# Masked keys' weight subtracted from P, and one product per head with v's totals, in a fused attention and FFN kernel

## The reference

```
x = x + LN(attn(LN(x)))          # x: (8, 512, 1024) float32
x = x + LN(ffn(LN(x)))

attn: qkv = x @ w_qkv.T + b_qkv  # 8 heads of 64, part = 512
      scores[f, t] = k[f] . q[t]             # no scaling
      scores = where(f <= t, scores, -10000)
      attn = softmax(scores, over f)
      vals[t] = sum_f attn[f, t] * v[f]
      out = vals @ w_o.T + b_o
ffn:  x @ W.T + b, plus the low-rank product B[:, :r] A[:r] x whose rank r (8, 16, 32, 64) the gate picks
```

## Time and profile before

| | |
|---|---|
| median of 3 runs | 1454.88 us (1454.22 to 1455.05) |
| span of the profiled execution | 1453.0 us |
| TensorE busy | 1436.8 us (99%) |
| VectorE, ScalarE, GpSimd busy | 920.2, 692.4, 623.7 us |
| HBM traffic | 59 GB/s over the span |

### The profile page before, as it was taken

The page is one execution under the profiler, slowest core; times in us unless marked ns, Lnnn a source line. Parts: engine busy times, 40 slices in busy tenths (PEclk is TensorE's granted clock), DMA queues, the critical chain, the costliest instruction groups (busy, mean ns, idle before and its releaser), DMA issues.

```text
span 1453.0 us, 24689 instructions
## 1 busy us (share of the span) xinstructions
PE 1436.8 (99%) x7852; PEld 1280.6 (88%) x7852; DVE 920.2 (63%) x2118; ACT 692.4 (48%) x1497; POOL 623.7 (43%) x1154
## 2 busy tenths in 40 slices
PE   7999999999999999999999999999999999999998
PEld 6888888888888888888888889999999999999998
DVE  7576575675675775765855887655555555555554
ACT  6365465564574673654654763333333323333332
POOL 3353451461553452533622584444443344444442
PEclk9999999999999999999999999999999999999999
DMA  7212113113122122121122722322222222222211
GB/s 251 83 41 70 58 35 101 32 26 101 36 54 69 40 54 79 40 58 65 40 58 91 207 88 102 102 102 102 100 82 85 101 101 87 101 101 101 94 69 62
DMA packets 51540, 118.72 MB, mean 82 GB/s; under 512 B 5552, under 2 KB 22192, under 8 KB 51504
## 3 DMA queue, kind: packets, MB, share of 16 engines
q1 hardware_dynamic: 51504, 118.27, 25.7%
HBM read 60.06 MB, written 25.69 MB: 59 GB/s over the span
## 4 chain that ended last, share of the span: by engine, by line
PE 95%; DMA 1%; POOL 1%; DVE 1%; ACT 1%; issue 0%; POOLq 0%; DVEq 0%
PE ps_f L2036 26%; PE ps_o L1391 20%; PE ps_o L1422 12%; PE ps_o L1987 11%; PE ps_s L1443 5%; PE ps_t L1301 4%; PE ps_v L1275 4%; PE ps_o L1385 3%; PE ps_v L1276 2%; PE ps_f L2017 2%; PE ps_o L1345 1%; PE ps_x L2006 1%; PE ps_t L1391 1%; PE ps_t L1284 1%; DMA valsT<-vt 1%; POOL wagl L616 1%
## 5 line engine op out<-in xcount | busy, mean ns | idle before, releaser
L2036 PE MATMUL ps_f<-wagh,x2Th 128*128 128x364 f32 x768 | 255.1, 332 | 0.4 <-POOL wagl L616 0.4
L2036 PE MATMUL ps_f<-wagh,x2Tl 128*128 128x364 f32 x768 | 252.6, 329 | 0.0
L2036 PE MATMUL ps_f<-wagl,x2Th 128*128 128x364 f32 x768 | 252.5, 329 | 0.0
L1391 PE MATMUL ps_o<-xTh,wh 128*128 128x512 f32 x424 | 174.1, 411 | 0.0
L1391 PE MATMUL ps_o<-xTh,wl 128*128 128x512 f32 x424 | 166.8, 393 | 0.0
L1391 PE MATMUL ps_o<-xTl,wh 128*128 128x512 f32 x424 | 165.9, 391 | 0.0
L2036 PEld LDWEIGHTS ps_f<-wagh,x2Th 128*128 128x128 f32 x768 | 144.3, 188 | 2.0 <-POOL wagl L616 0.7
L2036 PEld LDWEIGHTS ps_f<-wagl,x2Th 128*128 128x128 f32 x768 | 144.7, 188 | 1.1
L2036 PEld LDWEIGHTS ps_f<-wagh,x2Tl 128*128 128x128 f32 x768 | 144.5, 188 | 0.0
L558 POOL TENSOR_TENSOR cw<-wm,cnt 128x4 f32<-128x4 f32 x64 | 12.9, 202 | 299.8 <-ACT pr L1061 299.8
L731 DVE TENSOR_TENSOR PT<-ps_t,PT 128x512 fp32r<-128x512 f32 (+1 forms) x192 | 109.6, 599 | 41.2 <-ACT PT L1026 39.2
(11 more groups left out here) (222 smaller groups left out, 3494.6 us busy)
## 6 DMA issues: line engine op xcount, KB each, us to landing
kst<-kst SPq DMA_DIRECT2D x64, 256.0 KB, 3.7
xt<-in_x SPq DMA_DIRECT2D x32, 512.0 KB, 4.0
x2r<-x2n SPq DMA_DIRECT2D x30, 512.0 KB, 2.9
xs<-in_x SPq DMA_DIRECT2D x24, 512.0 KB, 4.4
out<-x SPq DMA_DIRECT2D x23, 512.0 KB, 3.0
valsT<-vt SPq DMA_DIRECT2D x64, 128.0 KB, 2.3
vraw<-valsT SPq DMA_DIRECT2D x32, 256.0 KB, 3.4
raw<-in_wqkvT SPq DMA_DIRECT2D x12, 512.0 KB, 5.9
```

The lines of the kernel that those rows point to most:

```text
L1391: done = pe.matmul(ps[:, :], w[:, k, c:c + P], xT[:, k, :], start=(k == 0 and w is wh and xT is xTh), stop=(k == KD - 1 and w is wl), skip ...
L2036: last = pe.matmul(ps_f[:, g, 0:GW], a[:, k, :], w[:, k, cols], start=(k == 0 and a is xh and w is wagh), stop=False, skip_group_check=True)
```

## The change

The masked keys' weight is no longer laid out as blocks of P. For query t the sum over all keys of wn[t] * v[f] is wn[t] times v's total. So the visible P becomes P - wn[t], and wn[t] * total is added for all keys:

vals[t] = sum over the visible key tiles of (P[f, t] - wn[t]) * v[f] + wn[t] * sum over all f of v[f]

- `normalise` subtracts wn in its second operation (an operand from SBUF in place of the constant 1.0), and a drain stands ahead of it, since wn is made just before.
- `values` reads high rows at their visible columns only, as the low rows (512, 384, 256, 128), and ends with one product: `totals[:, h, :]` by the head's diagonal (384 columns). pv_done follows that product.
- `masked_weights`, `masked_spread`, wt_ready and wn_done go; `transpose_p`'s group 1 waits for nothing of its own.
- `diagonal` has two buffers, and waits for pv_done of the head two back.
- New, once a row: ScalarE copies v tile 0 to vsum, VectorE adds tiles 1 to 3 (ahead of each tile's low part in `v_lo`), `vsum_hi` (ACT) and `vsum_lo` (DVE) split vsum, `value_totals` (PE) multiplies ones by both parts into ps_t[1] in the middle of slot 2's first projection, `totals_hi` (ACT) and `totals_lo` (DVE) split the result.
- PT's layout becomes plain, the loop's code loses the split of projections in slots other than 2, and the kernel is built with dynamic_dma_scratch_size=1024.

```diff
             def weights(h, b):
                 pool.wait_ge(rden_ready, H + 1)
-                pool.tensor_tensor(wn[:, q, :], wm[:, q, :], rden[:, q, :], ALU.mult).then_inc(wn_done, 1)
+                pool.tensor_tensor(wn[:, q, :], wm[:, q, :], rden[:, q, :], ALU.mult)
             def diagonal(h, b):
-                pool.wait_ge(wn_done, H + 1)
-                pool.wait_ge(wt_ready, 1 + H)
-                pool.tensor_tensor(W_DIAGONAL.rearrange("p (i t) -> p i t", i=3),
+                pool.wait_ge(pv_done, H + 1)
+                pool.tensor_tensor(DIAGONALS[q].rearrange("p (i t) -> p i t", i=3),
...
             def normalise(h, b):
+                pool.drain()
                 for i in range(NT):
                     at = pr[:, q, S_OFF[i]:S_OFF[i] + (i + 1) * P]
-                    last = pool.tensor_scalar(at, at, rden[:, q, i:i + 1], 1.0, ALU.mult, ALU.mult)
+                    last = pool.tensor_scalar(at, at, rden[:, q, i:i + 1], wn[:, q, i:i + 1].bitcast(F32),
+                                              ALU.mult, ALU.subtract)
                 last.then_inc(p_ready, 1)
...
             def v_lo(t, b):
                 dve.wait_ge(v_high, 4 * b + t + 1)
+                if t > 0:
+                    dve.wait_ge(v_low, 4 * b + t)
+                    done = dve.tensor_tensor(vsum[:, :], ps_j[t % 2][:, :], vsum[:, :], ALU.add)
+                    if t == NT - 1:
+                        done.then_inc(vsum_ready, 1)
...
+            def vsum_lo(b):
+                dve.wait_ge(vsum_high, b + 1)
+                dve.tensor_tensor(vsum_l[:, :], vsum[:, :], vsum_h[:, :].bitcast(F32), ALU.subtract).then_inc(vsum_low, 1)
+
+            def totals_lo(b):
+                dve.wait_ge(totals_high, b + 1)
+                dve.tensor_tensor(totals[:, :, HD:2 * HD], ps_t[1][:, :].rearrange("p (h c) -> p h c", h=NH),
+                                  totals[:, :, 0:HD].bitcast(F32), ALU.subtract).then_inc(totals_low, 1)
...
                     if h < NH and h != BARE + 1:
                         scores_max(h, b)
+                    if h == 2:
+                        totals_lo(b)
...
-            def masked_spread(h, b):
-                act.wait_ge(t_full[1], 2 * (8 * b + h) + 2)
-                act.activation(W_SPREAD, ps_t[1][:, 0:3 * P].rearrange("p (n c) -> p n c", n=3), ACT.Copy)\
-                    .then_inc(wt_ready, 1)
+            def vsum_hi(b):
+                act.wait_ge(vsum_ready, b + 1)
+                act.activation(vsum_h[:, :], vsum[:, :], ACT.Copy).then_inc(vsum_high, 1)
+
+            def totals_hi(b):
+                act.wait_ge(totals_full, b + 1)
+                act.activation(totals[:, :, 0:HD], ps_t[1][:, :].rearrange("p (h c) -> p h c", h=NH), ACT.Copy)\
+                    .then_inc(totals_high, 1)
...
         def values(pe, h, b):
             H = 8 * b + h
             pe.wait_ge(t_lo, 3 * H + 3)
-            pe.wait_ge(wt_ready, 1 + H + 1)
             if h == 0:
                 pe.wait_ge(v_low, 4 * b + 4)
             pe.wait_ge(vals_ready, 1 + H)
             for j in range(NT):
-                pe.matmul(ps_v[:, :], v[:, j, h, :], HIGH_ROWS[j], start=(j == 0), stop=False, skip_group_check=True)
-                last = pe.matmul(ps_v[:, j * P:], v[:, j, h, :], LOW_ROWS[j], start=False, stop=(j == NT - 1),
-                                 skip_group_check=True)
-            last.then_inc(pv_done, 1)
-
-        def masked_weights(pe, h, b):
-            H = 8 * b + h
+                for rows in (HIGH_ROWS[j], LOW_ROWS[j]):
+                    pe.matmul(ps_v[:, j * P:], v[:, j, h, :], rows, start=(j == 0 and rows is HIGH_ROWS[0]), stop=False,
+                              skip_group_check=True)
             pe.wait_ge(d_ready, H + 1)
-            pe.wait_ge(t_lo, 3 * H + 2)
-            pe.matmul(ps_t[1][:, 0:3 * P], ones[:, 0:1].to_broadcast([P, P]), W_DIAGONAL,
-                      start=True, stop=True).then_inc(t_full[1], 1)
+            if h == 0:
+                pe.wait_ge(totals_low, b + 1)
+            pe.matmul(ps_v[:, 0:3 * P], totals[:, h, :], DIAGONALS[h % 2], start=False, stop=True,
+                      skip_group_check=True).then_inc(pv_done, 1)
+
+        def value_totals(pe, b):
+
+            pe.wait_ge(vsum_low, b + 1)
+            pe.wait_ge(t_lo, 3 * 8 * b + 2)
+            for part in (vsum_h, vsum_l):
+                last = pe.matmul(ps_t[1][:, :], ones[:, 0:1].to_broadcast([P, P]), part[:, :],
+                                 start=(part is vsum_h), stop=(part is vsum_l))
+            last.then_inc(totals_full, 1)
```

More of the change, by code:

```diff
@@ L235, in attention_phase @@
         PT = sb("PT", [P, ROOM * P], F32R)
+        totals = sb("totals", [P, NH, 2 * HD], F32R)
+        vsum = sb("vsum", [P, PART], F32)
+        vsum_h = sb("vsum_h", [P, PART], F32R)
+        vsum_l = sb("vsum_l", [P, PART], F32R)
         ones = sb("ones", [P, 2], F32R)
@@ L676, in gpsimd @@
             pool.memset(hold[:, 1:2], 0.0).then_inc(vals_ready, 1)
-            pool.memset(hold[:, 14:15], 0.0).then_inc(wt_ready, 1)
+            pool.memset(hold[:, 14:15], 0.0).then_inc(pv_done, 2)
             pool.memset(hold[:, 2:3], 0.0).then_inc(vals_stored, 16)
@@ L879, in body @@
                         lows(h, 1, b)
+                    if h == 1:
+                        vsum_lo(b)
                     if 1 <= h <= NH and h not in (BARE, BARE + 1):
@@ L1066, in vals_lo_part @@
                 H = 8 * b + h
-                act.wait_ge(pv_done, H + 1)
+                act.wait_ge(pv_done, H + 3)
                 act.wait_ge(vals_ready, 1 + H)
@@ L1109, in body @@
                 for h in range(SLOTS):
-                    if h >= 2:
-                        masked_spread(h - 2, b)
+                    if h == 2:
+                        totals_hi(b)
                     if h == BARE + 2:
@@ L1157, in last_body @@
                 v_hi(3, b)
+                vsum_hi(b)
                 p_hi(0, 2, b)
-                masked_spread(0, b)
+                totals_hi(b)
                 exps(2, b)
@@ L1169, in last_body @@
                 p_hi(1, 2, b)
-                masked_spread(1, b)
                 q_hi(2, b)
@@ L1181, in last_body @@
                 tile_vals_high(1)
-                masked_spread(2, b)
                 q_hi(3, b)
@@ L1190, in last_body @@
                 next_high(W.wag[0])
-                masked_spread(3, b)
                 next_high(W.wag[1])
@@ L1201, in last_body @@
                     next_high(W.wag[k])
-                masked_spread(4, b)
                 exps(6, b)
@@ L1211, in last_body @@
                 next_high(W.wag[4])
-                masked_spread(5, b)
                 for k in (5, 6):
@@ L1484, in steps @@
                 items = between(BETWEEN_LAST if last else BETWEEN, h, part, b)
-                if part == 0 and h >= 2 and len(items) == 1:
+                if part == 0 and h == 2:
                     kind, p, row, ks = items[0]
@@ L1489, in steps @@
                     step(kind, p, row, ks, last)
-                    if n == 0 and part == 0 and h >= 2:
-                        masked_weights(pe, h - 2, b)
+                    if n == 0 and part == 0 and h == 2:
+                        value_totals(pe, b)
             def turns(h, place, b):
@@ L1519, in last_body @@
             def last_body(b):
-                whole, first, second = range(W.KV), range(W.KV // 2), range(W.KV // 2, W.KV)
+                whole = range(W.KV)
                 scores(0, b)
@@ L1525, in last_body @@
                     else:
-                        tile_product(h - 5, 1, first)
-                        masked_weights(pe, h - 2, b)
-                        tile_product(h - 5, 1, second)
+                        tile_product(h - 5, 1, whole)
                     if h >= 2:
@@ L1541, in last_body @@
                         transpose_p(pe, h - 1, 2, b)
-                tile_product(3, 1, whole[:1])
-                masked_weights(pe, NH - 2, b)
-                tile_product(3, 1, whole[1:2])
+                tile_product(3, 1, whole[:2])
                 values(pe, NH - 2, b)
@@ L2040, in ffn @@
                             last_transposes(pe)
-                        if first and g == 2 and k == 2:
-                            last_weights(pe)
                         if first and g == 2 and k == KD // 2:
@@ L2118, in _ @@
             attention.tensor(pe)
-            output.tensor(pe, attention.last_transposes, attention.last_weights, attention.last_values)
+            output.tensor(pe, attention.last_transposes, attention.last_values)
 def kernel(L0_attn_x, L0_attn_w_qkv, L0_attn_b_qkv, L0_attn_w_o, L0_attn_b_o, L0_ffn_W, L0_ffn_b, L0_ffn_A,
```

51 lines of the change are left out of this document (23 added, 28 removed).

## The result

| | time, us (median) | against the kernel before, 95% interval |
|---|---|---|
| before | 1454.55 (1453.91 to 1455.05) | |
| changed | 1587.47 (1584.39 to 1589.6) | 1.0913 (1.09 to 1.0926) |

A forecast was written before the change was run, and what follows sets the result against it. TensorE's own stream bounds the kernel: 11.0 us won without waits, but waits lose 0.22 us a row, 1.5 in seven rows, plus 1.2 in the last: 2.7 slower, 1457.6 us, range 1449 to 1462.

The forecast's parts named there:

- stage 2: GpSimd's normalise(): drain and second SBUF operand make P 0.47 us later; heads 5 and 7 wait, 0.95 us a row.
- 0.08 for each operand, and 4 x 0.07 to 0.08 = 0.28 for a head: Price of normalise()'s second SBUF operand on GpSimd, from 693 ns with one such operand against 611 with none.
- Most heads have several times that in slack: Claim that P being ready 0.47 us later delays TensorE's first transposes only in heads 5 and 7.
- The stream: TensorE's values and product of a head cost 1.43 us instead of 1.67, winning 14.7 us in 64 heads.
- value_totals(): Two added TensorE matmuls of 512 columns once a row: 0.46 us, in eight rows 3.7 us.
- The wait at the totals: TensorE waits for vsum_lo before the totals' product: 0.47 us a row, bounds 0.2 and 0.9.
- The wait at the product of head 0: TensorE waits for totals_lo at the product with the diagonal: about 0.2 us a row.
- P later: Later P from GpSimd: drain 0.18 to 0.2 us, operand 0.28 a head; head 5 waits 0.63, head 7 0.32.
- The last row: GpSimd's unbroken chain to the last wagl is pushed back by three normalisations: about 1.2 us slower (0 to 1.5).
- The sum: Seven rows lose 0.22 us each, 1.5 us, and the last row 1.2: 2.7 us slower, 1457.6 us.
- What would make the prediction wrong: Signs against the forecast: a TensorE stream without gaps (then 1444), or a short matmul costing more than 0.11 us.
- the 0.02 that was left for things not seen: Chance of 0.02 left beside the forecast and its rivals for outcomes that none of them covers.

The follow-up runs named there:

- a_rest: The changed kernel with normalise() as before (multiply by rden and by an immediate 1.0), so no subtraction from P, drain kept: 1455.43 us, 1.0008.
- a_order2: The changed kernel with P as (add a negated w, multiply by rden), both from SBUF, and without the drain: 1456.88 us, 1.0018.
- a_add: The changed kernel with normalise() as multiply by rden, then add of a negated weight, two small GpSimd instructions more a head: 1463.60 us, 1.0062.
- a_nototals: a_order2 without vsum, its parts, value_totals()'s products and the totals' parts; a totals tile of zeros is multiplied by the diagonal: 1447.21 us, 0.9952.
- best2: a_order2 with vsum made earlier, GpSimd's last x subtraction behind head 5's normalisation, q's parts ahead of head 1's values: 1453.79 us, 0.9998.
- b_sub0: The kernel before, with normalise() multiplying by rden and then subtracting an immediate 0.0 instead of multiplying by 1.0: 1538.53 us, 1.0578.
- b_subfirst: The kernel before, with normalise() first subtracting an immediate 0.0, then multiplying by rden: 1536.8 us (one run).
- best4: best2 with three more orders changed on VectorE, ScalarE and GpSimd, and the totals product moved to second place except in head 0: 1450.60 us, 0.9974.

## Why the prediction was wrong

The step that failed is one term of stage 2: "0.08 for each operand, and 4 x 0.07 to 0.08 = 0.28 for a head". It measured 3.6 us a head (5.69 against 2.06). With it goes "Most heads have several times that in slack", which was said of 0.47 us: TensorE waits for P in four heads of a row, 10.3 us together by the views, where I had 0.95 in two. I priced the second operand and took the operation for free, because the two rows I compared differ in an operand and not in the operation. No row of before has a subtraction in a tensor_scalar on GpSimd: those of lines 551, 581 and 593, and two small ones, add and multiply. The subtraction of line 596 is a tensor_tensor. Its 1.29 us beside the addition's 1290 ns at the same width (line 1709 of the changed kernel, below) would have told me that subtracting is cheap, and misled me:

```profile
L1709 POOL TENSOR_TENSOR x<-xt,z 128x512 f32<-128x512 f32 x46 | 58.3, 1290 | 0.9 <-ACT z L1879 0.9
```

An operation that the trace doesn't show has to be bounded from both sides. I gave the operand a bound and the operation none. Even GpSimd's slowest row for 512 columns (1.29 us, line 596) as the upper end would have missed 2.07, but the range would have been open upwards by up to 2.4 us a head (4 x 0.6), and a rival would have stood there: TensorE waits for P in most heads.

The Trainium skill ("GPSIMD Engine Reference", section "4.1 Engine selection") calls GpSimd's elementwise add, multiply and max on one input "roughly line-rate", and names no subtraction there. No run here shows what the line rate is. The rows show that a subtraction isn't to be read into that line: 512 columns take 693 ns with two multiplications and 1997 with a subtraction in place of one.

The other steps can be read in a_rest and a_order2, the kernels nearest to the change without that term (a_order2 also lacks the drain):

- The stream (timeline of a_rest). Values and product of a head: 1.44 us, 1.43 forecast, 0.22 less than before; 64 heads win 14 us, and the totals' products take 4.5 of them. Two terms were off against each other. The two 128-column matmuls take 0.06 and 0.11 rather than 0.11 each, and the product is followed at 0.23, not 0.17.
- value_totals(). Its first matmul is followed at 0.34 (476.91 to 477.25), not 0.23, so 0.56 us a row and not 0.46. In all the totals cost 9.7 us; 3.7 + 4.6 was forecast. Right, a little low.
- The wait at the totals. 0.54 us in a_rest, 0.47 forecast. The wait at the product of head 0 was 0.08 there, 0.2 forecast. Right.
- P later. The drain costs 0.18 ahead of line 548, as forecast; the operand 0.36, not 0.28. Head 5 was the one with no slack, and head 7 the next, as forecast: in a_add, where P is latest, head 5 waits 0.91 us (1.14 from start to start, as 527.38 to 528.52, less 0.23) and head 7 0.34; forecast 0.63 and 0.32. In a_order2 head 5 waits 0.54 and head 7 doesn't wait.
- Missed: the scores of head 4 wait about 0.38 us a row, at line 1432, and the values of head 6 about 0.2. I had looked at slack for P and for the totals, not for scores. a_nototals shows that the totals don't cause it. best2 shows that the chain through head 1's values and q's two parts does; that this chain was not late before because the stream ahead of it was longer is argued, not shown.
- The last row. Wrong in sign. From head 5 of the seventh row (726.70 before, 730.42 in a_order2) to the matmul that waits for the last wagl (857.93 and 860.03) a_order2 takes 1.6 us less, where 1.2 more were forecast. That matmul waits 0.77 us instead of 0.41; so the chain on GpSimd is longer, but not by all that the stream wins. Why isn't shown.
- The sum. It gave 2.7 us; a_order2 costs 2.7 by the medians. That agreement is luck, of two errors against each other: a row loses 0.57 us (two of them take 525.03 to 730.42, 102.7 us each, against 102.1) and not 0.22, with head 7 not waiting and the two missed waits in its place; and the last row wins 1.6 us where 1.2 were to be lost. a_add, which keeps the drain, costs 9.2.
- "What would make the prediction wrong" named a stream without gaps and a dear short matmul. It did name the row to look at, line 581 at 0.77 us for 512 columns, and that row was the one that failed.
- The clock. A cost that no rival had, since none had a wait above about 1 us: after a wait of 4.76 us TensorE ran at the lower clock. The result fell in the 0.02 that was left for things not seen. In a_order2, with waits of some tenths, the granted clock stays at 1.00.

```profile
100.00:800.00 700.00, 692.70 (x3655) 587.81 (x3654) 484.72 (x985) 379.93 (x942) 323.35 (x654) 1.00 0.21 58
```

## What to carry to other kernels

Price an operation by a row with the same instruction, engine, operand kinds and the same operation; a new operation in an old instruction is an unknown, and one run with that word changed and nothing else is the cheapest experiment there is. On GpSimd write a - b in a tensor_scalar as an addition of the negated scalar. In a kernel whose TensorE never waits, the order of the other engines is tuned to tenths of a microsecond: a shorter stream wins little until each chain behind it is shortened too (in a_order2 the waits had eaten the 9.5 us that the stream wins, and 2.7 more; seven changes of order won back 6, and an eighth lost 7).

## What the runs showed of the hardware

- GpSimd's tensor_scalar on float32 with a subtraction in either place: 737, 1150, 1604 and 1997 ns for 128 to 512 columns, 0.42 us for each 128 (b_sub0, b_subfirst); with two multiplications 371 to 693 ns, 0.11 us for each 128 (before). With a second scalar from SBUF 2074 ns for 512 columns (multiply, subtract) against 826 to 830 for the pairs without a subtraction. A tensor_tensor subtraction is not slow: 1.29 us for 512 columns, as an addition.
- A second scalar from SBUF adds 0.08 us at 128 columns (0.10 behind the drain, in a_add) and 0.13 at 512, nearly the same for (multiply, multiply), (multiply, add) and (add, multiply): 826, 830, 827 ns.
- After 4.76 us without work TensorE's granted clock was 0.50, and matmuls of 512 columns followed each other at 0.46 us; from 605.34 on they were back at 0.23. The clock was 0.50 after the wait of 3.32 us at head 7 too.
- Transposes start 0.23 us behind a 384-column matmul (a_rest); the same 384-column matmul is followed by another matmul at 0.17 (best4). Behind a 128-column matmul they start at 0.06 us in the kernel before, where a 512-column one stands ahead of it, and at 0.11 in best4, where a 128-column one does.
